# Edge tables before the layer norm, another order on the load queue, staggered key steps, and three scatter accumulators in DRAM

## What is computed

```
xn = layernorm(x)                                   # 6250 x 256
gathered = edge_weight[:, None] * xn[dst]           # 100000 x 256
new_x = segment_sum(gathered, src, 6250)            # scatter-add by src
out1 = tanh(batchnorm(new_x @ hamilton1))           # graph branch
gnn = out1 @ hamilton2
q, k, v = split(xn @ w_qkv)                         # attention branch, 8 heads of 32
kv = einsum(layernorm(k), layernorm(v)) / 6250
mix = gelu((q @ kv + xn) @ w1 + b1) @ w2 + b2 + xn
x = x + gnn + mix
```

## Time and profile before

| | us |
|---|---|
| median of 3 runs (lowest, highest) | 2470.51 (2464.07, 2475.68) |
| the profiled execution's own time | 2471.89 |
| its span in the trace | 2470.5 |
| preparation, until the first put | 174 |
| edges, first to last put | 1247 |
| nodes, until the first expert matmul | about 349 |
| experts and the copy to the output | about 700 |

### The profile page before, as it was taken

How to read it: one execution, slowest core, us unless ns; L and a number is a source line. 1 busy time by engine, 2 the same in 40 slices (tenths; PEclk the granted TensorE clock), 3 DMA queues, 4 the chain that set the end, 5 groups by cost and what they waited for, 6 DMA issues and landing times. The chain is left out here.

```text
span 2470.5 us, 38103 instructions
## 1 busy us (share of the span) xinstructions
PE 1955.3 (79%) x11227; PEld 1622.0 (66%) x11251; DVE 1738.6 (70%) x5437; ACT 1129.2 (46%) x2236; POOL 1289.5 (52%) x811
## 2 busy tenths in 40 slices
PE   2238888577888887878798546796799999999995
PEld 2126565356666565566687323675499999999995
DVE  6347767777885775767343157777888888888884
ACT  2013334222233223233333201523899989999983
POOL 3115555377888878888788800000155444554442
PEclk9669999788999888989899779755699999999997
DMA  8955445377779778887999776123288888888885
GB/s 292 379 175 84 75 74 82 67 118 120 128 129 184 120 126 159 136 167 128 193 209 198 106 222 198 65 79 124 79 237 230 235 235 229 231 238 229 236 235 163
DMA packets 332265, 414.86 MB, mean 168 GB/s; under 512 B 35129, under 2 KB 273358, under 8 KB 331796
## 3 DMA queue, kind: packets, MB, share of 16 engines
q1 hardware_dynamic: 200238, 263.26, 34.2%
q0 software_dynamic: 103008, 103.83, 30.8%
q10 hardware_dynamic: 28806, 45.26, 5.7%
HBM read 257.54 MB, written 161.10 MB: 169 GB/s over the span
## 5 line engine op out<-in xcount | busy, mean ns | idle before, releaser
L1074 POOL DMA_INDIRECT acc_dram<-third x566 | 923.5, 1632 | 420.4 <-issue 252.6
L1991 POOL DMA_INDIRECT sum_dram<-node,small x112 | 196.8, 1758 | 315.6 <-DVE node L1920 261.6
L1848 PE MATMUL bank<-up_parts 128*128 128x256 f32 x2688 | 334.5, 284 | 2.4 <-DVE up_parts L1878 2.4
L1861 PE MATMUL bank<-down_parts 128*128 128x256 f32 x2688 | 335.4, 284 | 0.0
L1848 PEld LDWEIGHTS bank<-up_parts 128*128 128x128 f32 x2688 | 329.2, 193 | 2.8 <-DVE up_parts L1878 2.8
L1861 PEld LDWEIGHTS bank<-down_parts 128*128 128x128 f32 x2688 | 325.3, 191 | 0.0
L542 PE MATMUL bank<-work,third 128*128 128x256 f32 x1132 | 302.7, 414 | 14.9 <-ACT third L1027 14.9
L1027 ACT ACTIVATE third<-bank 128x512 f32<-128x512 f32 x283 | 166.3, 597 | 274.8 <-DMA acc_dram<-third 219.9
L1973 POOL DMA_INDIRECT node<-xh_dram,small x112 | 137.7, 1230 | 248.4 <-DVE small L1674 214.6
L542 PEld LDWEIGHTS bank<-work,third 128*128 128x128 f32 x1132 | 227.5, 213 | 49.5 <-ACT third L1027 15.1
L836 DVE TENSOR_TENSOR third<-work,third 128x512 f32<-128x512 f32 (+1 forms) x142 | 97.2, 684 | 194.3 <-DMA work<-src_dram 194.3
(11 more groups left out here) (268 smaller groups left out, 3298.7 us busy)
## 6 DMA issues: line engine op xcount, KB each, us to landing
turned<-in_w_up SPq DMA_DIRECT2D x56, 1024.0 KB
turned<-in_w_down SPq DMA_DIRECT2D x56, 1024.0 KB
work<-src_dram SPq DMA_DIRECT2D x141, 256.0 KB
acc_dram<-fixed SPq DMA_DIRECT2D x20, 1280.0 KB, 14.8
work<-acc_dram SPq DMA_DIRECT2D x96, 256.0 KB, 3.9
work<-xn_dram SPq DMA_DIRECT2D x146, 128.0 KB
at_dram<-turned ACTq DMA_DIRECT2D x48, 256.0 KB
work<-at_dram ACTq DMA_DIRECT2D x24, 512.0 KB
```

The source lines that it names most:

```text
L1074: e.indirect_dma_start(acc_dram[i], bass.IndirectOffsetOnAxis(put_i[:, t:t + 1], 0), M[:, t % (2 * QUAD), :], None, compute_op=ALU.add).th ...
L1848: k = e.matmul(ps, W1s[:, 2 * b + wp, q, h * P:(h + 1) * P], xTs[:, 2 * b + xp, q, :], start=(q == 0 and (wp, xp) == TERMS[0]), stop=(q == ...
L1861: k = e.matmul(bank[5 + c][:, 0:D], hTs[:, hp, h, c * P:(c + 1) * P], W2s[:, 2 * b + wp, h, :], start=(h == 0 and hp == 0 and wp == 0), st ...
L1991: e.indirect_dma_start(sum_dram, bass.IndirectOffsetOnAxis(slot_i[:, n:n + 1], 0), yb[:, i % 2, c, :], None, compute_op=ALU.add).then_inc( ...
```

## The change

- `N_ACC` 4 to 3: three accumulators, 15 fills, a put waits for the third put before it. Put 0 to 3 all go to accumulator 0, put 4 to 11 to accumulators 0 and 1, from put 12 on all three are used (`EARLY`). In the node stage SP loads three tiles a pair of nodes and DVE adds half of what it did at L1468.
- DVE and PE build the edge tables ahead of the layer norm.
- SP: `src_dram` is stored as soon as the table exists; five fills (accumulator 0) go between the `xn` stores; then the first four spreads, three windows, the ten other fills, and the quads. The 32 loads of `w_gnn` go behind the last quad. `xnT` is no longer stored by ACT in one DMA of 6272 KB but by SP in 13 pieces, one in each of the turns 8 to 20.
- The spread ring is four deep and runs one quad further ahead.
- Keys: one step a tile that works on five tiles at once (copy of tile i, sum and centre of i-1, square and variance of i-2, root, inverse and scale of i-3, product of i-4) instead of four steps of one tile. New costs and `MIX_FIRST` 0: from the cost tables, keys stand beside quads 0 to 31 (one or two tiles a quad), mix and dense steps beside 32 to 112, products beside 113 to 137.

```diff
-N_ACC = 4
+N_ACC = 3
-MIX_FIRST = 10
+MIX_FIRST = 0
-EARLY = 12
+EARLY = (4, 12)
-        acc_of = [None] * T0 + [t % (N_ACC - 1) if t < EARLY else t % N_ACC for t in range(ET - T0)]
+        acc_of = [None] * T0 + [t % (1 + sum(t >= n for n in EARLY)) for t in range(ET - T0)]
...
-        costs = [0.7] * (1 + 4 * NT + 2) + [(1.7, 1.2)[which] for which in in_turn] + [2.6] * (2 * PRODUCTS)
+        costs = [2.0] + [2.8] * (NT + 4) + [1.0] * 2 + cost_in_turn + [2.4] * (2 * PRODUCTS)
...
         def keys_scalar(e):
-            for t in range(NT):
-                e.wait_ge(s_kvp, t + 1)
...
-                e.activation(kvs[:, t % 2, :], bank[5][:, :], ACT.Copy).then_inc(s_kvcp, 1)
-                yield
-                e.wait_ge(s_kvln, 5 * t + 2)
-                e.activation(kvq, kvd, ACT.Square).then_inc(s_kvsq, 1)
-                yield
-                e.wait_ge(s_kvln, 5 * t + 3)
-                e.activation(kve, kvar, ACT.Sqrt, bias=eps_col, scale=1.0 / HD).then_inc(s_kvsq, 1)
+            for i in range(NT + 4):
+                t = i - 2
...
+                    e.activation(kvq, kvn[:, t % 4, :], ACT.Square).then_inc(s_kvsq, 1)
+                t = i - 3
...
+                    e.activation(kve[:, t % 2, :], kvar2[:, t % 2, :], ACT.Sqrt, bias=eps_col, scale=1.0 / HD).then_inc(s_kvsq, 1)
+                if i < NT:
...
+                    e.activation(kvs[:, i % 2, :], bank[5][:, :], ACT.Copy).then_inc(s_kvcp, 1)
...
             e.wait_ge(s_set, SET_ZEROS)
+            e.wait_ge(s_split, 1)
+            e.dma_start(src_dram.rearrange("(g t) j -> t g j", t=P), src_f).then_inc(s_srcd, 16)
             for c in range(G):
+                if c < 5:
+                    fill(c)
                 e.wait_ge(s_xn, b)
                 e.dma_start(xn_dram[...], xn_ring[:, c % 2]).then_inc(s_xnd[c % 2], 16)
-                if c:
-                    fill(c - 1)
-            for n in range(G - 1, 5 * N_ACC):
-                fill(n)
...
-            for q in range(3):
+            for q in range(4):
                 spread(q)
...
+            for n in range(5, 5 * N_ACC):
+                fill(n)
             for q in range(NQ - 3):
-                spread(q + 3)
+                if 8 <= q < 8 + NCH:
+                    lo, hi, w = chunk(q - 8)
+                    e.wait_ge(s_xnT, NT)
+                    e.dma_start(xnT_dram[:, :, lo:hi], xnT[:, :, lo:hi]).then_inc(s_xnTd, 16)
+                if q + 4 < NQ:
+                    spread(q + 4)
                 window(q + 3)
...
-                e.tensor_tensor(sums[:, 0:2, 0:n * D], sums[:, 0:2, 0:n * D], sums[:, 2:4, 0:n * D], ALU.add).then_inc(s_accs, 1)
+                e.tensor_tensor(sums[:, 0, 0:n * D], sums[:, 0, 0:n * D], sums[:, 2, 0:n * D], ALU.add).then_inc(s_accs, 1)
```

More of the change, by code:

```diff
@@ L162, in gps_layer @@
         third = region("third", NT * D, late)
-        work = region("work", 12992, late)
+        work = region("work", 13064, late)
         src_c = third(EG * P)
@@ L336, in some @@
                 next(steps, None)
+        KEY_DONE, ROOT_DONE = {}, {}
+        for i in range(NT + 4):
+            for name, t in (("sum", i - 1), ("centre", i - 1), ("variance", i - 2), ("inverse", i - 3), ("scale", i - 3)):
+                if 0 <= t < NT:
+                    KEY_DONE[name, t] = len(KEY_DONE) + 1
+            for name, t in (("square", i - 2), ("root", i - 3)):
+                if 0 <= t < NT:
+                    ROOT_DONE[name, t] = len(ROOT_DONE) + 1
         dense_uses = []
@@ L703, in dense_vector @@
             vec.wait()
-            vec.done(e.tensor_reduce(least[:, 1:2], bad, AX.X, ALU.add))
+            vec.done(e.tensor_reduce(least_d[:, 1:2], bad, AX.X, ALU.add))
             for a, b, s in DENSE:
```

245 lines of the change are left out of this document (128 added, 117 removed).

## The result

The changed kernel takes **2379.52 us** (median of 4 runs, 2373.23 to 2384.72) against 2473.1 for the kernel before beside it: ratio 0.9611, 95% interval 0.955 to 0.9673. The forecast was 2377, so the sum is right to 2.5 us. It is right because large errors of opposite sign stand in it, which the stages show: a late start (26 us) and longer mix quads (23 us) against shorter key quads (29 us) and nodes (11 us).

The account below looks back on a forecast made before the run. POOL's puts were taken to bound most of the edge stage, the ACT-DVE ping-pong the key quads, late spreads the start. From 2470.5 us, 84 off the edge stage and 9 off the nodes gave 2377 us, range 2330 to 2428.

Parts of the forecast that it names:

- The start, gain 65 us: Start of edge stage: put 12 comes at about 139 us instead of 204, gain 65 us (50 to 75).
- its gain is on SP: the spreads now follow the last `xn` store: SP's queue at the start: spreads follow the last store at 87 us, first put at 100 (95 to 115).
- 40 us, just covered by the same 139: Puts 0 to 11 on one, then two accumulators: 4 to 7 us per landing, 40 us, not delaying put 12.
- Keys, 263 us: Quads 3 to 30: PE becomes the bound instead of the ping-pong, 9.4 us a quad, 263 us (213 to 342).
- Rival 4: Better: higher PE clock, keys at 8.4 us a quad, no density cost, half the landing term saved; 2330 us, chance 0.13.
- Mix quads, 663 us: 80 quads of mix and dense steps: 647 us at the old pace, plus density and landings, 663 us.
- but less covers a late step, so 8 us: Mix quads: PE and DVE stay below 8.09 us a quad, yet denser steps cost 8 us (0 to 48).
- Three accumulators, 23 us: Puts held where landings pass 5.6 us: 15 us in the products, 8 before, 23 us (0 to 120).
- Nodes, 9 us: Node stage: half-size add at L1468 saves 6 us, fewer loads for the first three pairs 3 us; 9 us.
- The start is eaten: Early puts land slowly behind ten fills and stall the quads; start gains 15 us instead of 65, 2427 us, chance 0.07.
- lockstep: Key steps still wait on each other between engines: 11 us a quad, 2422 us, or 12.2, 2456 us; chance 0.11.
- slower: Landings on the third accumulator set the pace of 430 POOL-bound puts; 2514 us at 7.1 us a landing, chance 0.05.

Follow-up runs that it names:

- c: Changed kernel with the old start: layer norm ahead of edge tables, all 15 fills ahead of the source-list store, three accumulators from put 0; 2368.96 us.
- g1: c with five more fills of the same size in SP's row, into a tensor nothing reads; 2399.2 us (one run).
- g2: c with `xnT` stored at once by ScalarE ahead of its mixing work, instead of 13 pieces from SP; 2392.03 us (one run).
- g3: c with the edits of g1 and g2, the `w_gnn` loads ahead of SP's loop and three key steps ahead of quad 0; 2406.69 us.
- c2: Changed kernel, tables still ahead of the norm, but with SP's row as in c and three accumulators from put 0; 2392.7 us (one run).
- b: Changed kernel with the earlier kernel's key steps, four steps of one tile, spread over the same 28 quads; 2426.95 us.
- a: Changed kernel with the fourth accumulator back from put 36, its five fills one per turn in quads 0 to 4; 2381.56 us.
- d: Changed kernel with planner cost 2.2 instead of 2.8 for a key step, so keys end earlier and later steps spread over more quads; 2376.83 us.
- j: i with a fourth accumulator from put 44 on, its five fills one per turn in quads 5 to 9; 2368.37 us.
- i: Changed kernel with `x` loads of groups 1 to 6 behind edge lists, ten fills beside the norm, five in quads 0 to 4, third accumulator from put 24; 2371.22 us.
- k: Changed kernel with `x` loads of groups 1 to 6 behind edge lists, all 15 fills beside the norm, three accumulators from put 0; 2368.32 us.

## Why the prediction was right, and where it was not

- **The start, gain 65 us: wrong by 26, and wrong in its reason.** The step that failed is "its gain is on SP: the spreads now follow the last `xn` store". They do (92.55), and the first put came at 108.4, inside 95 to 115. But "40 us, just covered by the same 139" failed: puts on one accumulator under ten fills were 8.3 to 10.6 us apart and not 4 to 7, and the tables began at 29.69 because the last edge list landed behind `x`, not 4 us after its issue. The gain came from the bytes on the queues and not from their new order: c reaches put 12 at 151.5 with the old order, and g1 and g2 show that five fills (17.6 us) and the `xnT` store (15.2 us) had kept the kernel before waiting. These are 32.8 of the 52.7 us between c and the kernel before; 10.2 more came back in g3 unseparated, and 9.7 stay open. I had looked only at what stands ahead of what, and credited neither the dropped fills nor the store that moved behind quad 8. The new order was a loss: tables ahead of the norm cost 21 us by themselves (c2), of which the new order of SP's queue won 7.6 back.
- **Keys, 263 us: right in mechanism, 29 too high.** PE was the next bound as said, busy 95%, and b shows that the stagger is what makes it so. The term that was mis-sized is PE's work: I took 47 tiles beside quads 3 to 30, and the trace has 168 matmuls of L410, 42 tiles (about 17 us), as five tiles stand beside quads 0 to 2; the quads' own matmuls took 85.2 us and not 28 x 3.45 = 96.6, at a granted clock of 0.96 against 0.93. The split of PE's time into 3.45 us a quad and 3.37 a tile was rough from the start: the lines of PE in the earlier trace rows's window overlap and add up to 250.9 us where PE was busy for 214.06, and I took the quads' share from the one and the sum from the other. Rival 4 had the 8.4 us.
- **Mix quads, 663 us: 23 too low.** The landings cost 13 us here (686.1 against 673.1 in a) and not 8, which leaves 686 - 647 - 13 = 26 for density where I had 8. This is the term that was mis-sized. Both engines did stay below 8.09 us a quad (PE 560.56/80 = 7.01, DVE 6.02); the step that failed is what I drew from it, "but less covers a late step, so 8 us". In d PE was busy for 23.3 us less in these 80 quads and they were 22.7 us shorter; the kernel before had 6.62 us of PE work a quad, 0.38 less, and quads 0.33 shorter when the landings are left out. So PE's work came out nearly whole, although PE was busy for 82% only. That is a comparison and not a mechanism: with the same steps a has 9.7 us less of PE's busy time, and no run separates the new costs of the mix and dense steps or the deeper spread ring. My upper bound of 48 us "if all of the denser PE work lay bare" does not follow from its own numbers either, which give 80 x (7.0 - 6.6) = 32.
- **Three accumulators, 23 us: right size.** a shows 29.3 in the edge stage (13 in the mix quads, 17 in the products, where I had 8 and 15), j 33.8 from quad 10 on. POOL's waits for landings behind quad 33 are 48.9 us by their own row, but about 90 with the 41 us that are put down to copies long done, over the 60 that I had named; a shows that they cost only 30 us of time. The Trainium skill ("DMA: Bandwidth & Descriptors", section "Anatomy of one DMA — SWDGE (gpsimd) path") gives 2.0 us and the bytes at 436 GB/s, by which I had estimated a landing 3.9 us after the start, too early to hold a put. The trace does not agree: where a copy of ACT waited for a put behind quad 33 (95 times), it began 3.9 to 14.3 us after the later put of its pair had started, and over 5.6 us after it in 53 of the 95.
- **Nodes, 9 us: 20 measured.** The half-size add was sized right (671 ns for 0.68 us), but I let it count in half of the pairs. The adds of 25 pairs came 3.62 us apart instead of 4.14, so it was all of them, some 12.5 us; a shows 17 us for this edit alone. The rest of the 20 is open.
- **The rivals.** "The start is eaten" was half true (26 of its 50 us, and by its mechanism, the ring of 8 tiles that stalls the quads), "better" was true of the keys, lockstep and "slower" did not happen. Had the errors of the start (26) and of the keys (29) had one sign, they would have moved the sum by 55 us, to 2322 or 2432, both outside the range of 2330 to 2428. That the sum came out to 2.5 us is luck; the stages were right to 20 or 30.

## What to carry to other kernels

When work waits behind a row of large transfers, add up the bytes of all queues ahead of it before reading the order: while the DMA engines were full here, a transfer that was dropped or went past the busy stretch helped by its whole time, and a store on another engine's queue counted like one on this. The order comes after that, and can still lose 20 us when it delays what the transfers wait for (c2). A result that agrees with a forecast says little of its terms; undo the parts one by one. When a row of waits names an engine, see whether that engine had been done long before: then the wait was for something else, here for a landing. And a buffer that is given up in one stage (an accumulator) is paid where transfers land late and earned where its data are read back, so both stages belong in its price.

## What the chip showed that I had not expected

- POOL stood idle for 6.8 to 9.0 us before each of puts 1 to 4, waiting for the put before to land while 1280 KB fills moved, against at most 0.7 us in the kernel before, with more accumulators and no fill in the way. With one fill issued ahead of a quad's puts (i) such waits were 4.6 to 5.0 us.
- Fills of zeros into DRAM ran at 376 GB/s (1310720 bytes in 3.49 us); the mix of loads, stores and fills of i and k kept 348 to 376 GB/s for 60 us and more. A store issued by ScalarE (6272 KB) lengthened SP's row by 14.8 us.
- PE's granted clock in the key quads (a mean over the stretch, as a share of the upper level of 2.4 GHz) was 0.93 with PE busy for 83%, 0.96 at 95% (changed), 1.00 at nearly 100% (d), and the mean of a key matmul 637, 620 and 603 ns. In b it was 0.96 at 86%, with a mean of 652 ns, so these three do not go together in every run.
